# Attention, router and mixture-of-experts layer on one core: the last expert weights sent in pieces during attention, one address read moved ahead of a wait, one root moved ahead of a copy

## What is computed

```python
def attn(x):                       # b=2, s=2048, d=256, 16 heads of 16
    q, k, v = split(x @ Wq), split(x @ Wk), split(x @ Wv)
    scores = (q.k + lam * (q_cos.k_cos + q_sin.k_sin)) * scale   # causal
    return softmax(scores) @ v @ Wo

def ffn(X):                        # NE=8 experts, 256 -> 512 -> 256
    gating = softmax(X @ Wg + bg);  top 2 experts of each row
    h = silu((X @ W1 + b1) * (X @ W3 + b3))
    expert_outputs = h @ W2 + b2
    mixed = sum(topk_w * expert_outputs of the two)
    return mixed @ Wf + bf

x = layernorm(x + attn(x))
x = layernorm(x + ffn(x))
```

## Time and profile before

| | |
|---|---|
| median of 3 runs | 1855.59 us (1855.54 to 1859.55) |
| the profiled execution | 1852.48 us |
| its span, first to last instruction | 1850.7 us |
| PE busy | 1694.5 us, 92% |
| DVE busy | 1266.7 us, 68% |
| ACT busy | 887.9 us, 48% |
| mean granted clock of PE | 0.967 |
| attention's last value sum ends | about 1290.8 us |
| first load of expert rows issued | 1335.76 us |
| loads of finish begin | 1773.18 us |

### The profile page before, as it was taken

How to read it: one execution, slowest core, us unless ns; L and a number is a source line. 1 busy time by engine, 2 the same in 40 slices (tenths; PEclk the granted TensorE clock), 3 DMA queues, 4 the chain that set the end, 5 groups by cost and what they waited for, 6 DMA issues and landing times.

```text
span 1850.7 us, 28030 instructions
## 1 busy us (share of the span) xinstructions
PE 1694.5 (92%) x8956; PEld 871.3 (47%) x8957; DVE 1266.7 (68%) x3117; ACT 887.9 (48%) x1036; POOL 347.4 (19%) x484
## 2 busy tenths in 40 slices
PE   6999989999999999999999989997189999999955
PEld 3544444444444444444444444442145666666644
DVE  3589887787787877787887767864355555555545
ACT  2876665655555555556565545556111222222235
POOL 0000021121111212212221221223323111111112
PEclk9999979999999999999999989999599999999988
DMA  3465434020020122121220300523821111111153
GB/s 109 159 222 197 162 136 157 7 97 21 20 91 8 52 93 79 64 81 42 87 86 14 107 33 1 178 71 121 291 96 42 45 46 46 46 46 46 43 163 127
DMA packets 105203, 163.30 MB, mean 88 GB/s; under 512 B 11516, under 2 KB 65548, under 8 KB 104712
## 3 DMA queue, kind: packets, MB, share of 16 engines
q1 hardware_dynamic: 89560, 126.63, 20.7%
q0 software_dynamic: 15536, 35.28, 5.7%
HBM read 91.84 MB, written 69.27 MB: 87 GB/s over the span
## 4 chain that ended last, share of the span: by engine, by line
PE 72%; ACT 5%; DVE 5%; DMA 4%; issue 3%; SPq 1%; POOL 0%; DVEq 0%; ACTq 0%; POOLq 0%
PE att_ps_s L1162 22%; PE exp_ps_h L1891 13%; PE att_ps_o L1181 12%; PE att_ps_m L275 10%; PE exp_ps_y L1909 7%; DMA att_sums<-att_out_t 3%; ACT att_probs L1221 3%; DVE att_maxima L285 2%; PE exp_ps_t L1899 2%; PE att_ps_m L1583 1%; PE fin_ps_y L1400 1%; PE exp_ps_x L1880 1%; ACT L1221 0%; PE pre_ps_h L498 0%; PE pre_ps_q L498 0%
## 5 line engine op out<-in xcount | busy, mean ns | idle before, releaser
L1221 ACT ACTIVATE att_probs<-att_ps_s 128x1024 f32<-128x1024 f32 (+3 forms) x640 | 561.9, 895 | 448.1 <-PE att_ps_s L1162 440.7
L1162 PE MATMUL att_ps_s<-att_queries,att_keys 49*128 49x512 f32 (+3 forms) x2560 | 619.6, 555 | 29.6 <-ACT att_probs L1221 22.0
L285 DVE TENSOR_REDUCE att_maxima<-att_ps_m 128x1 f32<-128x512 f32 x768 | 486.9, 683 | 111.3 <-PE att_ps_m L275 107.8
L275 PE MATMUL att_ps_m<-att_keys,att_queries 48*128 48x512 f32 (+3 forms) x1280 | 481.4, 576 | 12.2 <-DVE att_maxima L285 4.9
L275 PEld LDWEIGHTS att_ps_m<-att_keys,att_queries 48*128 48x128 f32 x1280 | 190.3, 185 | 302.0 <-DVE att_maxima L285 149.9
L1162 PEld LDWEIGHTS att_ps_s<-att_queries,att_keys 49*128 49x128 f32 x2560 | 238.3, 189 | 146.4 <-ACT att_probs L1221 102.2
L288 DVE CUSTOM_DVE_ANT_0 att_ps_m<-att_ps_m,att_future 128x128 f32<-128x128 f32 (+3 forms) x512 | 240.9, 512 | 71.4 <-PE att_ps_m L275 70.3
L1181 PE MATMUL att_ps_o<-att_probs,att_values 128*32 128x512 f32 (+3 forms) x2560 | 270.0, 536 | 1.1 <-POOL att_probs L1299 1.1
L1891 PE MATMUL exp_ps_h<-keep_w,exp_rows_t 128*128 x568 | 258.8, 599 | 10.7 <-DVE exp_rows_t L1925 10.7
L1967 ACT ACTIVATE exp_hidden<-exp_product 128x512 f32<-128x512 f32 x71 | 44.8, 631 | 352.1 <-DVE exp_product L1950 352.1
L1299 POOL TENSOR_SCALAR_AFFINE_SELECT att_probs<-att_probs 128x512 f32<-128x512 f32 x128 | 83.2, 650 | 400.5 <-ACT att_probs L1221 400.1
(11 more groups left out here) (194 smaller groups left out, 1390.0 us busy)
## 6 DMA issues: line engine op xcount, KB each, us to landing
att_queries<-q_parts SPq DMA_DIRECT2D x64, 192.0 KB
att_keys<-k_parts SPq DMA_DIRECT2D x64, 192.0 KB
exp_rows<-sorted_rows SPq DMA_DIRECT2D x71, 129.0 KB, 2.3
v_rows<-pre_v_sb SPq DMA_DIRECT2D x8, 1024.0 KB, 4.6
q_parts<-pre_waves SPq DMA_DIRECT2D x16, 512.0 KB, 5.2
k_parts<-pre_waves SPq DMA_DIRECT2D x16, 512.0 KB, 6.2
att_values<-v_rows SPq DMA_DIRECT2D x32, 256.0 KB
keep_w<-in_L_ffn_W_dram SPq DMA_DIRECT2D x4, 2048.0 KB, 16.7
```

The lines of the kernel that those rows point to most:

```text
L275: pe.matmul(bank[:, 0:width], self.queries[g % 2][half, c, r, P * q:P * q + P], self.keys[g % 2][half, k, r, 0:width], start=True, stop=Tr ...
L285: dve.tensor_reduce(to, bank[:, 0:width], AX.X, ALU.max).then_inc(self.s_mr, 1)
L1162: mm = pe.matmul(score_tile(unit, first, last)[:, e], keys[g % 2][half, k // TPC, r, P * (k % TPC):P * (k % TPC) + P].bitcast(F32), querie ...
L1221: act.activation(probs[:, step % PROBS, DUO * r:DUO * r + DUO, first:last], score_tile(unit, first, last), ACT.Exp, scale=SCALE).then_inc( ...
```

## The change

Three edits. The order of instructions on PE, DVE and POOL is untouched.

1. The six last weight transfers become seven, and are issued at three times. The first six experts' part of b3 (1.5 MB) goes out after the last chunk's `load`, once the scores have begun on the last chunk of queries and all maxima ahead of it are taken. W2 blocks 2 and 3 and b1 go out ahead of the own moves, each once `s_pv` says that its ring places have been read for the last time (steps 314, 315 and 317, counted from 0). W2 blocks 0 and 1 and the last two experts' part of b3 (0.5 MB) stay behind the own moves.
2. SP reads the address of the first tile ahead of its wait for the puts.
3. In finish, ACT's root for chunk i - 3 stands ahead of the copy for chunk i - 1.

```diff
             routing.load(sp, NCH - 1, s_store, s_kept)
+            sp.wait_ge(s_scores, units_done((QUADS - 1) * STEPS + FIRST[QC - 1]) - len(units_of(0)))
+            sp.wait_ge(s_mr, sum(MAX_TILES[n % QC] for n in range(CHUNKS - 1)))
+            sp.dma_start(*under_queries).then_inc(routing.s_last, 16)
             routing.keep_rows(sp, NCH - 2)
+            last_of = lambda place: max(step for step in range(QUADS * STEPS) if step % PROBS == place)
+            for places, load in sorted(later, key=lambda item: max(map(last_of, item[0]))):
+                if max(map(last_of, places)) < QUADS * STEPS - 2:
+                    sp.wait_ge(s_pv, max(map(last_of, places)) + 1)
+                    sp.dma_start(*load).then_inc(routing.s_last, 16)
             routing.move_own(sp, out_t[:, (CHUNKS - 1) % 2], range(QUAD))
             sp.wait_ge(s_pv, QUADS * STEPS)
             sp.wait_ge(s_scores, QUADS * len(UNITS))
-            for to, rows in later:
-                sp.dma_start(to, rows).then_inc(routing.s_last, 16)
+            for places, load in later:
+                if max(map(last_of, places)) >= QUADS * STEPS - 2:
+                    sp.dma_start(*load).then_inc(routing.s_last, 16)
+            sp.dma_start(*over_keys).then_inc(routing.s_last, 16)
             routing.keep_rows(sp, NCH - 1)
...
             sp.wait_ge(routed.s_edge, 16)
+            ahead = entry(sp, tile_in, 0, NE * REGION_TILES)
             for i in range(2):
                 sp.wait_ge(routed.s_put[i], routed.rows_put)
...
-                sp.dma_start(rows[:, p], at(rows_in, entry(sp, tile_in, s, NE * REGION_TILES))).then_inc(s_x[p], 16)
+                first = ahead if isinstance(s, int) and s == 0 else entry(sp, tile_in, s, NE * REGION_TILES)
+                sp.dma_start(rows[:, p], at(rows_in, first)).then_inc(s_x[p], 16)
...
-            pipelined(act, NCH, [(normalise, 4), (weigh_first, 0), (keep_mixed, 1), (lambda i, p: norm.root(act, i, eps[:, 0:1]), 3)])
+            pipelined(act, NCH, [(normalise, 4), (weigh_first, 0), (lambda i, p: norm.root(act, i, eps[:, 0:1]), 3), (keep_mixed, 1)])
...
-        later = weight_blocks(w2, W2) + biases[1:]
+        later = [((k,), load) for k, load in enumerate(weight_blocks(w2, W2))] + [((HK, HK + 1), biases[1])]
+        seen = 2 * (QC - 1)
```

More of the change, by code:

```diff
@@ L1044, in load, with attend @@
                      self.rows_v[row, :, :, g % NQ * QUAD * VW:(g % NQ + 1) * QUAD * VW]).then_inc(arrived, 16)
[L1047 removed]
+def attend(nc, block, small, features, quads, highest, made, out_parts, inv_rows, first_weights, biases, later, under_queries, over_keys, routing):
     plan = Plan().made()
@@ L2170, in program @@
         biases = [(to[:, :].rearrange("p e h -> p (e h)"), rows.rearrange("e h -> (e h)").partition_broadcast(P))
-                  for to, rows in ((bias2, b2), (bias1, b1), (bias3, b3))]
+                  for to, rows in ((bias2, b2), (bias1, b1))]
+        half_3 = lambda part: (bias3[:, part].rearrange("p e h -> p (e h)"), b3[part].rearrange("e h -> (e h)").partition_broadcast(P))
         attention = ExitStack()
```

5 lines of the change are left out of this document (2 added, 3 removed).

## The result

The changed kernel takes 1847.2 us in the median of 6 runs (1845.37 to 1851.81), the kernel before 1857.3 in 6 runs on the same chip (1855.54 to 1859.95). The profiled execution took 1845.37 with a span of 1843.6, where that of before had 1852.48 and 1850.7.

What follows compares the result with a forecast made beforehand. Though PE was 92% busy, it took pads queued behind weights to bound the attention-to-experts gap, and PE's loop to bound finish. Terms -4.9, 0 and -3.4 sum to -8.3, so 1855.6 becomes 1847.3 us, range 1842.5 to 1853.2.

Steps and rivals of the forecast that it cites:

- Early weights at no cost: End of attention: b3's early part costs nothing, and W2 blocks and b1 leave the own moves' issue at 1296.87.
- rival of the full queue: Ahead of the own moves: early issues stall in SP's queue, delay 13.0 us, total 1859.4; chance 0.05.
- Own moves late by 0.9: Attention to experts: 4 MB of weights ahead in SP's queue delay the last own move's landing by 0.9 us.
- Stall of the fourth pad gone: Pads before the experts: the fourth's 2.90 us issue falls to the usual 0.33, last pad issued at 1326.1.
- The landing of 4.0: Before the experts: last pads and puts land in 4.0 us, bounds 2.60 and 6.2; SP released 4.9 us earlier.
- What is late next: At SP's release before the experts: pads land last at 1330.1, the last put 0.6 us ahead at 1329.5.
- Address: nothing forecast: Before the first expert load: the early read stays behind the pads' wait, gain 0; better bound 0.65 us.
- experts "keep their length": Expert stage to 1771: starts earlier, but its length is unchanged because PE's loop sets it.
- Finish 3.4: In finish, root ahead of copy: gap 1.0, chunk 3's product 1.7 and tail 0.7 us gained.
- clock falls all the same: Rival in finish: chunk 3's product stays slow, 6.6 us gained in all, total 1849.0; chance 0.10.
- rival of pads slow among themselves: Before the experts: pads and puts, not weights, slow the landing; it stays at 7.2 us, total 1850.5; chance 0.14.
- own moves waiting 6.8 longer: Rival between attention and experts: own moves delayed 6.8 us in place of 0.9, total 1853.2; chance 0.11.

Runs made afterwards that it cites:

- all_three: The changed kernel measured once more, on the same chip as the single edits; 1848.65 us, ratio 0.9961 to the kernel before.
- weights_only: The kernel before with the first edit alone, the weights sent early; 1850.53 us, ratio 0.9971.
- spare_copy: The changed kernel with one or two unread copies on ACT ahead of the copy for chunk 3 in finish; 1848.48 and 1857.07 us, one execution each.
- dose run: Another name for b3_after_b1.
- b1_late: The changed kernel with b1 sent behind the own moves; 1849.39 us, ratio 0.9945 to the kernel before.
- address_only: The kernel before with the second edit alone, the first tile's address read ahead of the wait for the puts; 1861.67 us, ratio 1.0023.
- b3_after_b1: The changed kernel with the early part of b3 moved from behind the row load to right ahead of the own moves; one execution took 1849.68 us.
- root_only: The kernel before with the third edit alone, the root ahead of the copy in finish; 1852.94 us, ratio 0.9986.
- own_from_act: The changed kernel with the own moves issued by ACT in place of SP; 1850.43 us, ratio 0.9966 to the kernel before.

## Why the prediction was right, point by point

The sign, the likeliest case and the time came out: 1847.2 for 1847.3 forecast. Part of that closeness is luck. The kernel before stood at 1857.3 in the comparison and not at the 1855.6 that the forecast starts from, so the change brought 9.7 (all_three: 7.2) where the sum said 8.3, and two terms erred against each other.

**Early weights at no cost: right.** No early issue stalled (0.65, 1.63, 0.34), and b1 went out 8.15 ahead of the first own move, where the prediction had 1288.7 against 1296.87, 8.17. The rival of the full queue didn't occur.

**Own moves late by 0.9: right mechanism, size 0.9 forecast and 1.2 on average.** 1.7 in the profile of after (5.91 against 4.19), 0.9 and 0.8 in weights_only and all_three. The two spare_copy traces add 0.8 and 1.6. The dose run took it to 5.1 and b1_late to 0.4. "Last own move landing near 1301.8" came out as 1306.92; 4.3 of that is attention, which ended later, and from the first own issue it is 5.77 where 4.9 was said. By its letter the prediction's own sign of failure, "an own move landing after 1304", came true; it was tied to a clock time that attention moves, and with the 4.3 taken off the landing is at 1302.6. Most of the wait is for busy engines: in a queue of their own the own moves were late by 1.3, through SP under the same load by 1.6. The prediction had put it to the place in SP's queue. Its remark that the puts, in POOL's queue, don't wait for the weights doesn't hold for the last chunk: its eight puts took 6.5 to 9.0 to land in before, with the weights under way, and 2.6 to 3.3 in after.

**Stall of the fourth pad gone: right.** No issue of 2.9 is left. The eight pads' issues took 8.73 and 8.74, so from the first issue to the last 8.41 where 9.1 was said: the last four reads between the issues (L1761) took 0.52 to 0.66 in before, 0.33 to 0.45 in after.

**The landing of 4.0: the term that was mis-sized.** In the ten traces with early weights the last pad lands in 2.1 to 2.8 and the last put in 2.6 to 3.1; the lower bound of the prediction, 2.60 from the first expert load, was the right row, and the puts under four routing loads were not like this place. The estimate of 2.3 from the Trainium skill ("DMA: Bandwidth & Descriptors", section "Anatomy of one DMA") agrees with the trace's 2.38 to 2.5 for a pad; that section's formula is a fit to transfers that GpSimd issues, and the pads are SP's, so this is agreement of a number and not a test of the formula.

**"What is late next" came out the other way round.** The prediction had the pads last by 0.6, and the put is last by 0.37. Two things turned it. The pads' issues took 0.7 less than forecast and the puts' did not, so the last put is issued behind the last pad (1330.78 after 1330.61), where it was to be 0.6 ahead; and a put lands more slowly (2.6 against 2.38), where both were to take 4.0.

**Address: nothing forecast, 0.3 to 0.6 found.** The condition in the text ("hidden only if the last put lands after the last pad") is right in kind, and address_only confirms its other half: with the pads last, nothing. It left out that the read is hidden only as far as the put comes behind the pad. What failed in the forecast is the order of landing.

The gap as a whole, from the profile of before: the pads' first issue to the load was to be 13.9 (1317.0 to 1330.9) and took 11.62. Of the 2.3 less, 0.7 is issue and 1.6 the landing of the last pad (2.38 in place of 4.0). The read behind it is on the path as it was; had it stood behind the put as well, the load would have gone out 0.3 later (1333.36 + 0.80 = 1334.16). The own moves took back 0.8 and the projection 0.1. So 6.2 in place of 4.9; against the mean of the four kernels without the edit (38.4) the five traces with the change's placing (mean 32.6) are 5.8 shorter.

**The experts "keep their length": wrong by about 1.** From the first load to the start of finish's first product the four kernels without the weight edit take 448.5 to 449.4, mean 449.0, the ten traces with it 447.3 to 448.3, mean 447.9. Half a microsecond is the first load, which brings PE its first rows 2.14 to 2.23 after its issue in place of 2.18 to 3.25. The other half is the first expert product, 5.1 to 6.1 in place of 5.3 to 6.7, which starts at a granted clock of 0.50; whether the edit has a part in that isn't shown. The 1.9 in the table of the first section has 0.2 more from the product of chunk 0 in finish, which goes by the clock too.

**Finish 3.4: right where the clock falls, the cause half named.** Gap 0.92 (1.0 forecast), product 1.7, tail 0.7: 3.3. But the prediction said that the root's place ahead of the copy gives all of it. It gives the tail; the 2.6 come from the table load leaving PE's loop. And the 1.7 aren't always there to be gained: where the first product was the slow one, the gap cost 0.92 alone (35.38 against 34.46). The rival "clock falls all the same" was the wrong way round: after gaps of 1.10 to 1.18 it never fell in finish, and with the old order it fell in two traces of three.

The rival of pads slow among themselves fell with the landings; that of own moves waiting 6.8 longer didn't occur in after, but b3_after_b1 came to 5.1 with only the place of one 1.5 MB transfer changed, so it was a near neighbour.

## What to carry to other kernels

Bulk loads should be through, or not yet issued, when short dependent writes come: here 5.5 MB moved forward took the landing of the last such write from 6 or 7 to about 2.5 us, and the 2 MB of b1 did least harm behind the small transfer that PE waits for, not 8 us ahead of it. A table load belongs to a place where its engine is idle, whatever the order of the rest. And in a kernel whose length wanders by several microseconds, edits of 1 to 6 are told apart by stretches between fixed instructions, not by the total.

## What the runs showed of the hardware

**The end of attention has two lengths, about 2 us apart, and they go with the clock.** In the last steps of attention PE idles 1.82 for ACT in all 14 traces. In seven of them the next scores ran at a lower clock for longer, and the stretch from chunk 30's copy to the own moves took 65.7 to 66.2, in the seven others 63.5 to 63.9; its mean granted clock is 0.91 to 0.94 in the long ones and 0.95 to 0.96 in the short ones. It isn't the early weights: root_only has none, and 65.7, and four traces with them have 63.5 to 63.9. What decides between the two isn't shown. PE's timeline and a window of root_only, then the same place in before:

```profile
1279.88 6.10 PE L1162 MATMUL att_ps_s<-att_queries,att_keys 49*128 49x512 f32 x16 [1.82 <-ACT att_probs L1221]
```

```profile
1284.00:1288.00 4.00, 4.00 (x18) 0.50 0.00 0
```

```profile
1275.50 5.46 PE L1162 MATMUL att_ps_s<-att_queries,att_keys 49*128 49x512 f32 x16 [1.82 <-ACT att_probs L1221]
```

The granted clock is at 0.50, its level of 1.2 GHz, for the whole window, with no transfer at all beside it.

**The same issue by SP took 2.19 or 6.97, by what was sent shortly before it.** The last part of b3, issued right behind two W2 blocks, took 2.19 in after, where b1 had gone out 12 us earlier, and 6.97 in own_from_act, where b1 had gone out 5 us earlier; in b3_after_b1, with 3.5 MB sent 12 us earlier, it took 4.32. b1 itself took 0.34 in after, 5.3 after the end of the issue ahead of it.

**The same kernel, before, ran between 1850.15 and 1867.79** in 25 executions on one chip: a spread of 17.6 us, with the changes here worth 3 to 10. The time goes with the mean granted clock: the five shortest executions had 0.966 to 0.969, the five longest 0.959 to 0.962.
